# Expert tiles of 128 rows, the second matmul with the gelu's output stationary, its bias added at eviction

## The chip, the cores and the metric

The kernel runs on one core of a Trainium2 chip. The metric is the device time of one launch in microseconds. The array engine is TensorE (PE in the profile, its weight loads PEld), the others are VectorE (DVE), ScalarE (ACT), GpSimd (POOL) and SyncE (SP). A name with a q behind it (DVEq, SPq) stands for work of that engine's instruction sequencer: register arithmetic, waits, issues of DMAs.

## What is computed

Two transformer layers over 16 sequences of 256 tokens of width 128, in fp32. The first is attention with a band mask, then a mixture of experts; the second is attention with 16 small heads, then a recurrent cell. The change touches the mixture of experts alone:

```python
logits = -dist2 + x @ rw.T + rb              # 16 experts
topv, topi = lax.top_k(logits, 4)            # each token goes to 4 of them
w = softmax(topv)
hidden = gelu(x @ w1[e].T + b1[e])           # 128 -> 512
exp_out = hidden @ w2[e].T + b2[e]           # 512 -> 128
fused = sum over the 4 of w * exp_out
x = layernorm(x + fused)
```

## The kernel before

Each engine has its own program, written out by hand, and the engines meet at semaphores: `need(engine, name, count)` is a wait, `.then_inc` counts up. Loops are `batch_loop`, which writes the first and last turns out and leaves the middle to a loop of the engine's sequencer (its branch stands at L42).

The first stage is the attention of layer 0 with the routing. For each of the 4096 x 4 pairs of token and expert GpSimd scatters the token's row to `xs` in HBM, into the region of its expert. When all are counted, VectorE works out a plan (L1190 to L1231): the experts' regions are cut into tiles of GT = 256 rows, and for every tile `plan` holds the expert's number and the first row. The number of tiles is fixed, NT = 80, and those past the end run on a dummy region. SyncE and ScalarE write zeros behind each expert's last row (`pad`, L346). Meanwhile the weights of all experts lie in the on-chip array `wall`, per expert 516 columns of w1 and b1 (WA) and 513 of w2 and b2 (WB).

The expert stage then runs over tiles n. In a turn of the loop each engine does:

- SyncE: `load_rows(n + 2)`, 256 rows from `xs` to `xg`, after reading the row's number from `plan` (L389).
- TensorE: four matmuls up(n), w1 stationary and 256 columns of `xgT` moving (L766); two transposes of the rows of tile n + 1 (L748); four matmuls down(n - 1), w2 stationary and `hid` moving, into the bank DN (L774); two transposes of `yTe` of tile n - 2 back to rows (L780).
- ScalarE: four gelus of tile n (L993), then `yTe` = DN + b2, b2 being one value per partition (L997), then the store of tile n - 3 from `yrow` to `ys` (L984).
- VectorE: reads the expert's number of tile n + 1 from `plan` (L1240), copies its part of `wall` to `wA` (L1243), copies the transposed rows from PSUM to `xgT` (L1250), copies `wB` (L1246), and copies the rows of tile n - 2 from PSUM to `yrow` (L1291).

`wA`, `wB`, `hid`, `xg` and `yrow` have two buffers each. SyncE loads eight constants for the last stage (`cw_in`) in its first turn, and TensorE waits for them ahead of its second turn of the loop (L755). Behind the second turn VectorE runs `prepare()` (L1257), which ends with the comparison at L1271 that GpSimd waits for; GpSimd then rewrites positions and clears buffers, and clears one more (`clear(2)`, L532) once the last `wB` is copied, since that buffer lies inside `wall`. When `ys_out` says that all rows are stored, GpSimd gathers the rows of `ys` (L543), and the attention of layer 1 starts.

## Time and profile before

| | |
|---|---|
| median of 3 launches | 1743.43 us |
| lowest and highest | 1741.2 and 1749.72 us |
| span of the profiled execution | 1814.1 us |
| PE busy | 1434.0 us (79%) |
| PEld busy | 974.1 us (54%) |
| DVE busy | 1064.9 us (59%) |
| ACT busy | 973.5 us (54%) |
| POOL busy | 448.9 us (25%) |
| L766, 640 records, mean | 390 ns |
| L774, 640 records, mean | 379 ns |
| HBM read, written | 47.92 MB, 29.49 MB |

The profiled execution is 71 us longer than the median without a profile. For it only the span from the first to the last instruction is known, no launch time of its own. The table counts records: an fp32 matmul leaves two records and a transpose one. A record of a matmul has its end modelled, so the distance between starts tells more than the length.

### The profile page before, as it was taken

What the parts mean: (1) busy time and instruction counts of PE and PEld (TensorE: products, weight loads), DVE (VectorE), ACT (ScalarE), POOL (GpSimd) and SP (SyncE); (2) the same over time, 40 slices, a digit from 0 to 9 for tenths busy, and PEclk for the clock granted to TensorE, in tenths of its full rate; (3) what the DMA queues carried; (4) which work ended last, traced back from release to release, by engine and by line L of the source; (5) the groups of instructions that cost most, each with busy time, mean ns of one, the idle gap of its engine ahead of it and who ended that gap; (6) DMA issues with size and microseconds to landing.
All of it is one profiled execution on the core that took longest, in us unless ns stands there. A gap on an engine that the chain in (4) does not pass through costs nothing.

```text
span 1814.1 us, 32941 instructions
## 1 busy us (share of the span) xinstructions
PE 1434.0 (79%) x8094; PEld 974.1 (54%) x8094; DVE 1064.9 (59%) x3974; ACT 973.5 (54%) x2664; POOL 448.9 (25%) x495
## 2 busy tenths in 40 slices
PE   7999999999999999818999999125676667567581
PEld 4666665666665656416788888112344344335351
DVE  2677777777777777636443343025466556656555
ACT  6777777777777777414455555002344334334454
POOL 1012111222222212125100000665434433441003
PEclk9999999999999999859999999656788778878896
DMA  9000000000000000022122222144334333332301
GB/s 342 1 10 12 12 12 12 12 12 12 12 12 12 10 10 12 11 81 64 59 67 69 64 69 66 38 63 57 49 54 51 50 41 56 49 49 42 41 2 46
DMA packets 76443, 78.90 MB, mean 43 GB/s; under 512 B 10769, under 2 KB 69650, under 8 KB 75954
## 3 DMA queue, kind: packets, MB, share of 16 engines
q1 hardware_dynamic: 55378, 49.77, 13.9%
q0 software_dynamic: 8192, 16.79, 3.3%
q10 hardware_dynamic: 12816, 11.67, 1.9%
q8 instruction: 24, 0.39, 0.1%
q14 instruction: 33, 0.27, 0.1%
HBM read 47.92 MB, written 29.49 MB: 43 GB/s over the span
## 4 chain that ended last, share of the span: by engine, by line
PE 26%; DMA 11%; SPq 6%; issue 4%; DVE 3%; another core or an unknown queue 2%; ACT 1%; DVEq 1%; POOL 1%; POOLq 0%; ACTq 0%
PE psum L766 7%; PE psum L774 7%; DMA qst<-mrow 5%; SPq L425 3%; PE psum L810 3%; DMA wall<-mrow 3%; PE psum L799 2%; DMA qkd<-parts 2%; SPq L439 1%; PE psum L873 1%; PE psum L748 1%; PE psum L832 1%; PE psum L780 1%; POOL yk L543 1%
## 5 line engine op out<-in xcount | busy, mean ns | idle before, releaser
L947 ACT ACTIVATE P<-shifted,least 128x192 f32<-128x192 f32 (+1 forms) x512 | 240.9, 471 | 179.5 <-DVE least L1111 164.9
L1311 DVE TENSOR_REDUCE mx<-psum 128x2 f32<-128x512 f32 x256 | 165.6, 686 | 172.2 <-PE psum L873 128.3
L1010 ACT ACTIVATE wall<-psum 128x1024 f32<-128x1024 f32 x128 | 131.1, 1024 | 215.9 <-PE psum L799 153.2
L659 PE MATMUL psum<-kT,qT 128*128 128x384 f32 (+1 forms) x512 | 214.7, 542 | 0.0
L492 POOL DMA_INDIRECT xs<-x1c,pos x128 | 125.1, 978 | 335.2 <-DVE pos L1182 298.5
L1111 DVE CUSTOM_DVE_ANT_0 shifted<-psum,band 128x192 f32<-128x192 f32 (+1 forms) x512 | 170.6, 383 | 48.7 <-PE psum L659 32.9
L993 ACT ACTIVATE hid<-psum,wA 128x256 f32<-128x256 f32 x320 | 133.1, 471 | 66.3 <-PE psum L766 65.4
L766 PE MATMUL psum<-xgT,wA 128*128 128x256 f32 x640 | 157.5, 390 | 11.1 <-DVE xgT L1250 11.1
L674 PE MATMUL psum<-ident,P 128*128 128x128 f32 x1024 | 138.4, 278 | 18.7 <-DVE P L1104 18.6
L774 PE MATMUL psum<-hid,wB 128*128 128x256 f32 x640 | 151.4, 379 | 0.4 <-ACT yTe L997 0.4
L1104 DVE TENSOR_SCALAR P<-P,rinv 128x192 f32<-128x192 f32 (+1 forms) x512 | 145.1, 345 | 9.9
L674 PEld LDWEIGHTS psum<-ident,P 128*128 128x128 f32 x1024 | 116.2, 142 | 40.6 <-DVE P L1104 22.8
L543 POOL DMA_INDIRECT yk<-ys,posc x128 | 123.1, 962 | 48.9 <-issue 34.1
L766 PEld LDWEIGHTS psum<-xgT,wA 128*128 128x128 f32 x640 | 118.6, 195 | 26.7 <-issue 11.3
L774 PEld LDWEIGHTS psum<-hid,wB 128*128 128x128 f32 x640 | 115.5, 190 | 13.1 <-issue 0.6
L915 ACT ACTIVATE kT<-psum,cols 64x256 f32<-64x256 f32 x256 | 118.5, 463 | 3.2
L1246 DVE COPY wB<-wall 128x513 f32 x80 | 45.6, 570 | 126.0 <-ACT yTe L997 126.0
L659 PEld LDWEIGHTS psum<-kT,qT 128*128 128x128 f32 x512 | 95.8, 190 | 41.6 <-issue 1.4
L799 PE MATMUL psum<-qst,kst 128*128 128x256 bf16 x352 | 64.4, 315 | 57.3 <-DMA qst<-mrow 50.2
L947 ACT ACTIVATION_READ_ACCUMULATOR P<-shifted,least 128x1 f32 x512 | 95.6, 187 | 0.0
L1090 DVE TENSOR_TENSOR V<-psum,bv 128x512 f32<-128x512 f32 x62 | 42.8, 690 | 85.8 <-PE psum L619 61.3
L873 PE MATMUL psum<-kst,qst 128*128 128x256 bf16 x352 | 66.2, 314 | 30.1 <-DVE mx L1311 21.5
(244 smaller groups left out, 2649.6 us busy)
## 6 DMA issues: line engine op xcount, KB each, us to landing
xg<-xs SPq DMA_DIRECT2D x80, 128.0 KB, 2.0
ys<-yrow ACTq DMA_DIRECT2D x80, 128.0 KB, 1.7
wall<-in_wall SPq DMA_DIRECT2D x1, 8232.0 KB, 35.6
qkd<-parts SPq DMA_DIRECT2D x16, 384.0 KB
qst<-qkd SPq DMA_DIRECT2D x66, 64.0 KB
kst<-qkd SPq DMA_DIRECT2D x66, 64.0 KB
wall<-qkd SPq DMA_DIRECT2D x60, 64.0 KB
hT<-in_xT SPq DMA_DIRECT2D x4, 512.0 KB, 5.9
```

Source lines behind the costliest of these rows:

```text
L492: nc.gpsimd.indirect_dma_start(out=xs, out_offset=bass.IndirectOffsetOnAxis(pos[:, k:k + 1], 0), in_=x1c[:, k // TOPK, :], in_offset=None) ...
L543: g.indirect_dma_start(out=yk[:, n, :], out_offset=None, in_=ys, in_offset=bass.IndirectOffsetOnAxis(posc[:, n:n + 1], 0)).then_inc(s["yk_ ...
L659: mm(bk[:, 0:2 * w].rearrange("q (h j) -> q h j", h=2), qT[:, p, it * 128:(it + 1) * 128], kT[:, p, :, 0:w], start=True, stop=True).then_i ...
L674: last = nc.tensor.transpose(bk[:, c0:c0 + 128], P[:, par1, it, h, jt * 128:(jt + 1) * 128], ident[:, :])
L766: mm(UP[p][:, f * GT:(f + 1) * GT], wA[:, p, f * 128:(f + 1) * 128], xgT[:, p, :], start=True, stop=True).then_inc(s["up_mm"], 1)
L774: last = mm(DN[:, 0:GT], wB[:, q, f * D:(f + 1) * D], hid[:, q, f, :], start=(f == 0), stop=(f == FC - 1))
L947: last = sc.activation(P[:, par, it, h, 0:w], shifted[:, par, it, h, 0:w], ACT.Exp, scale=-1.0, bias=least[:, par, n:n + 1], accum_out=row ...
L993: sc.activation(hid[:, p, f, :], UP[p][:, f * GT:(f + 1) * GT], ACT.Gelu, bias=wA[:, p, F + f:F + f + 1]).then_inc(s["hid_ready"], 1)
L1010: sc.activation(pc[:, p % 4, :, :, :].rearrange("q h j n -> q (h j n)"), ST, ACT.Exp, scale=SCALE1).then_inc(s["exps1"], 1)
L1104: v.tensor_scalar(x, x, rinv[:, par1, n:n + 1], None, ALU.mult).then_inc(s["pn_ready"], 1)
L1111: v.tensor_tensor_reduce(out=shifted[:, par, it, h, 0:w], in0=bk[:, h * w:(h + 1) * w], in1=band[:, it, 0:w], scale=-SCALE0, scalar=3.0e38 ...
L1311: v.tensor_reduce(out=mx[:, :, h], in_=SB[(par + 1 + h) % 3].rearrange("q (i n) -> q i n", i=TT), axis=mybir.AxisListType.X, op=ALU.max).t ...
```

## The change

Tiles have 128 rows instead of 256, and NT is 144 instead of 80 (18,432 rows instead of 20,480). The loop is unrolled by four tiles, and `xg`, `wA`, `wB`, `hid` and `yrow` have four buffers. `yTe` and its transposes are gone: down(n - 2) has the gelu's output `hid` stationary and w2 moving, so rows of tokens come out, and DN has two banks. The bias b2 lies along the row there, so it is needed on all partitions: at the end of the first stage TensorE multiplies each expert's b2 column, broadcast to 128 columns, by the identity (16 products), and ScalarE copies the result into `wall` (4 copies), whose WB part grows from 513 to 640 columns. VectorE adds it while it moves DN to `yrow`. The stores go from ScalarE to SyncE, two tiles at a time. Pads write 128 rows, and the plan's arithmetic handles two columns of tiles.

The stages around it are otherwise the same. The diff, cut to its core:

```diff
-GT = 256
+GT = 128
-NT += NT % 2
+NT += -NT % 4
-WB = FC * D + 1
+WB = FC * D + D
```

SyncE:

```diff
-            load_rows(0, 0)
-            load_rows(1, 1)
+            def load_rows(n, buf):
+                need_alone(sp, "tin_mm", n - 3)
+                sp.dma_start(xg[:, buf, :], xs[bass.ds(row_of(n), GT), :]).then_inc(s[f"xg_in{buf}"], 16)
+            def store_rows(n, buf):
+                need_alone(sp, "yrow_ready", n + 2)
+                need_alone(sp, "ys_out", 8 * n)
+                sp.dma_start(ys[bass.ds(n * GT, 2 * GT), :].rearrange("(a p) d -> p a d", a=2), yrow[:, buf:buf + 2, :]).then_inc(s["ys_out"], 16)
+            for n in range(4):
+                load_rows(n, n)
             def body(i):
+                for p in range(4):
+                    n = 4 * i + p
+                    if is_tile(i, p, 4):
+                        load_rows(n + 4, p)
+                    if p % 2 == 1 and is_tile(i, p, -5):
+                        store_rows(n - 5, (p - 5) % 4)
                 if isinstance(i, int) and i == 0:
                     for dst, src in ((cw, "cw"), (lora_a, "lora_a"), (lora_b, "lora_b"), (gw, "gw"), (gu, "gu"), (gcol, "gcol"),
                                      (bo1, "bo1"), (bo2, "bo2")):
                         load(dst, src, "cw_in")
```

TensorE:

```diff
+            pe.wait_ge(s["wall_in"], 16)
+            for e in range(E):
+                b2 = wall[:, e, WA + FC * D:WA + FC * D + 1].to_broadcast([128, D])
+                mm(psum[:, e * D:(e + 1) * D], b2, ident[:, :], start=True, stop=True).then_inc(s["b2_mm"], 1)
...
+                    n, two = 4 * i + p, p % 2
                     if is_tile(i, p, 0):
                         need(pe, "xgT_ready", n + 1)
                         need(pe, "wA_ready", n + 1)
                         need(pe, "hid_ready", 4 * n - 4)
                         for f in range(FC):
-                            mm(UP[p][:, f * GT:(f + 1) * GT], wA[:, p, f * 128:(f + 1) * 128], xgT[:, p, :], start=True, stop=True).then_inc(s["up_mm"], 1)
+                            mm(UP[two][:, at:at + GT], wA[:, p, f * 128:(f + 1) * 128], xgT[:, two, :], start=True, stop=True).then_inc(s["up_mm"], 1)
                     if is_tile(i, p, 1):
-                        rows_in(n + 1, q, 16 * i + 16 * (p + 1))
-                    if is_tile(i, p, -1):
-                        need(pe, "yTe_ready", n - 1)
+                        rows_in(n + 1, (p + 1) % 4, 16 * (i + (p + 1) // 4) + 16)
+                    if is_tile(i, p, -2):
+                        need(pe, "hid_ready", 4 * n - 4)
+                        need(pe, "wB_ready", n - 1)
+                        need(pe, "yrow_ready", n - 3)
                         for f in range(FC):
-                            last = mm(DN[:, 0:GT], wB[:, q, f * D:(f + 1) * D], hid[:, q, f, :], start=(f == 0), stop=(f == FC - 1))
+                            last = mm(DN[two][:, 0:D], hid[:, m, f, :], wB[:, m, f * D:(f + 1) * D], start=(f == 0), stop=(f == FC - 1))
                         last.then_inc(s["dn_mm"], 1)
-                        for k in range(2):
-                            last = nc.tensor.transpose(TO[:, k * D:(k + 1) * D], yTe[:, p, k * 128:(k + 1) * 128], ident[:, :])
-                        last.then_inc(s["tout_mm"], 1)
```

ScalarE:

```diff
+            for k in range(0, E, 4):
+                act.wait_ge(s["b2_mm"], k + 4)
+                sc.copy(wall[:, k:k + 4, WA + FC * D:WCOLS], psum[:, k * D:(k + 4) * D].rearrange("q (e d) -> q e d", e=4))
             act.drain().then_inc(s["a_done"], 1)
...
-                        sc.activation(yTe[:, q, :], DN[:, 0:GT], ACT.Identity, bias=wB[:, q, FC * D:FC * D + 1]).then_inc(s["yTe_ready"], 1)
-                    if is_tile(i, p, -3):
-                        store(n - 3, q)
```

VectorE:

```diff
                     if is_tile(i, p, 1):
                         e = expert_of(n + 1)
                         need(dve, "up_mm", 4 * n)
-                        need(dve, "hid_ready", 4 * n)
+                        need(dve, "hid_ready", 4 * n - 8)
                         weights_A(e, q)
-                        rows_T(n + 1, q)
-                    if is_tile(i, p, -1):
-                        need(dve, "dn_mm", n)
-                        need(dve, "yTe_ready", n)
+                        rows_T(n + 1, q % 2)
+                    if is_tile(i, p, -2):
+                        m = (p - 2) % 4
+                        need(dve, "dn_mm", n - 1)
+                        need(dve, "ys_out", 16 * ((n - 4) // 2) if isinstance(n, int) else 32 * i + (16 * ((p - 4) // 2)))
+                        v.tensor_tensor(yrow[:, m, :], DN[p % 2][:, 0:D], wB[:, m, FC * D:FC * D + D], ALU.add).then_inc(s["yrow_ready"], 1)
                     if is_tile(i, p, 1):
+                        need(dve, "yrow_ready", n - 2)
                         weights_B(e, q)
-                    if is_tile(i, p, -2):
-                        need(dve, "tout_mm", n - 1)
-                        need(dve, "ys_out", 16 * n - 48)
-                        v.tensor_copy(yrow[:, p, :, :], TO[:, 0:GT].rearrange("q (a d) -> q a d", a=2)).then_inc(s["yrow_ready"], 1)
```

The order of VectorE inside the loop, before, from one copy into wB to the next copy of the rows and the wB behind it. `ISA` and `REGISTER_ALU` are steps of the sequencer, and the names in brackets are the semaphores that a step waits for:

```order
L1246 COPY wB<-wall 128x513
L294 REGISTER_ALU
L294 ISA [waits tout_mm]
L1291 COPY yrow<-psum 128x256 [waits ys_out]
L1240 ISA
L1240 TENSOR_LOAD plan
L1240 ISA x2
L294 REGISTER_ALU
L1243 ISA [waits hid_ready,up_mm]
L1243 COPY wA<-wall 128x516
L294 REGISTER_ALU
L1250 COPY xgT<-psum 128x256 [waits tin_mm]
```

And VectorE inside the loop after the change, from one yrow to the next wA:

```order
L298 ISA [waits dn_mm]
L1291 TENSOR_TENSOR yrow<-psum,wB 128x128 [waits ys_out]
L298 REGISTER_ALU
L1250 ISA [waits yrow_ready]
L1250 COPY wB<-wall 128x640
L1244 ISA
L1244 TENSOR_LOAD plan
L1244 ISA x2
L298 REGISTER_ALU
L298 REGISTER_ALU [waits up_mm]
L1247 ISA [waits hid_ready]
L1247 COPY wA<-wall 128x516
```

The copy into wB has moved behind yrow and waits for it, and the reading of `plan` (TENSOR_LOAD) now stands behind wB instead of behind yrow. The wait for ScalarE's yTe is gone.

TensorE inside the loop, one tile before the change:

```order
L294 ISA [waits wA_ready,xgT_ready]
L766 MATMUL psum<-xgT,wA 128x256 [waits hid_ready]
L766 MATMUL psum<-xgT,wA 128x256 x3
L294 REGISTER_ALU
L748 MATMUL psum<-ident,xg 128x128 [waits xgT_ready,xg_in0]
L748 MATMUL psum<-ident,xg 128x128
L774 MATMUL psum<-hid,wB 128x256 [waits yTe_ready,wB_ready,hid_ready]
L774 MATMUL psum<-hid,wB 128x256 x3
L780 MATMUL psum<-ident,yTe 128x128 [waits yrow_ready,yTe_ready]
L780 MATMUL psum<-ident,yTe 128x128
```

And one tile after it:

```order
L298 REGISTER_ALU
L298 ISA [waits wA_ready,xgT_ready]
L782 MATMUL psum<-xgT,wA 128x128 [waits hid_ready]
L782 MATMUL psum<-xgT,wA 128x128 x3
L764 MATMUL psum<-ident,xg 128x128 [waits xgT_ready,xg_in3]
L791 MATMUL psum<-wB,hid 128x128 [waits yrow_ready,wB_ready,hid_ready]
L791 MATMUL psum<-wB,hid 128x128 x3
```

One transpose and the two of yTe have gone, down waits for a yrow three tiles back and for no result of ScalarE that is newer than that of two tiles back, and up still waits for xgT and wA of its own tile.

## Rows read from the trace of the kernel before

**Rows 1.** Windows: length, busy time by engine (instructions), clock, DMA share, GB/s

```profile
900.00:920.00 20.00, 20.00 (x105) 17.34 (x104) 7.70 (x21) 11.26 (x27) 0.00 (x0) 1.00 0.23 70
```

**Rows 2.** Timeline of one tile: start, length, engine, line, count, idle before, releaser

```profile
950.37 0.42 DVE L1291 COPY yrow<-psum 128x256 f32<-128x256 f32 x1
...
951.24 1.89 PE L774 MATMUL psum<-hid,wB 128*128 128x256 f32 x8
...
951.40 0.43 DVE L1243 COPY wA<-wall 128x516 f32 x1 [0.61 <-ACT hid L993]
...
951.75 0.42 DVE L1250 COPY xgT<-psum 128x256 f32<-128x256 f32 x1
...
953.16 0.47 ACT L997 ACTIVATE yTe<-psum,wB 128x256 f32<-128x256 f32 x1 [1.11 <-PE psum L774]
...
953.18 1.89 PE L766 MATMUL psum<-xgT,wA 128*128 128x256 f32 x8
...
953.85 0.43 DVE L1246 COPY wB<-wall 128x513 f32 x1 [1.68 <-ACT yTe L997]
...
954.19 0.42 DVE L1291 COPY yrow<-psum 128x256 f32<-128x256 f32 x1
...
954.30 1.65 ACT L993 ACTIVATE hid<-psum,wA 128x256 f32<-128x256 f32 x4 [0.66 <-PE psum L766]
...
957.08 1.89 PE L766 MATMUL psum<-xgT,wA 128*128 128x256 f32 x8
```

**Rows 3.** Timeline: runs of 128-column fp32 records, two stages

```profile
500.37 1.04 PE L674 MATMUL psum<-ident,P 128*128 128x128 f32 x8
...
821.13 0.96 PEld L757 LDWEIGHTS psum<-lora_b,lora_a 16*128 16x128 f32 x8 [1.18 <-DMA bo<-in_bo]
```

**Rows 4.** L1240 in two tiles: count, min/median/max ns, first and last start

```profile
L1240 DVEq TENSOR_LOAD <-plan x1: 465/465/465, 950.4 to 950.4; - x1
...
L1240 DVEq TENSOR_LOAD <-plan x1: 321/321/321, 954.4 to 954.4; - x1
```

**Rows 5.** Groups of the page: busy, mean ns of one, idle before

```profile
L1090 DVE TENSOR_TENSOR V<-psum,bv 128x512 f32<-128x512 f32 x62 | 42.8, 690 | 85.8 <-PE psum L619 61.3
```

**Rows 6.** Timeline and L393: the start of the expert stage

```profile
809.27 0.42 DVE L1250 COPY xgT<-psum 128x256 f32<-128x256 f32 x1 [7.23 <-PE psum L748]
...
809.75 3.78 PE L766 MATMUL psum<-xgT,wA 128*128 128x256 f32 x8 [0.52 <-DVE xgT L1250]
...
822.21 1.99 PE L766 MATMUL psum<-xgT,wA 128*128 128x256 f32 x8
...
L393 SPq DMA_DIRECT2D xg<-xs x2: 342/364/387, 806.4 to 807.5; - x2
```

**Rows 7.** Timeline, windows and groups: preparation and the stretch with GpSimd

```profile
831.45 0.22 DVE L1259 CAST identb<-ident 128x128 bf16<-128x128 f32 x1
...
859.05 3.48 DVE L1243 COPY wA<-wall 128x516 f32 x1
...
858.64 3.61 POOL L504 MEMSET kst<- 3x4096 bf16 x1
...
835.90:869.40 33.50, 24.60 (x120) 20.32 (x120) 29.43 (x27) 12.90 (x30) 31.73 (x16) 1.00 0.14 47
...
L1246 DVE COPY wB<-wall 128x513 f32 x6 | 13.8, 2305 | 3.0 <-ACT yTe L997 3.0
...
L1243 DVE COPY wA<-wall 128x516 f32 x7 | 12.2, 1746 | 0.5 <-ACT hid L993 0.5
```

**Rows 8.** Windows and timeline: the end of the expert stage

```profile
1137.30:1144.70 7.40, 5.38 (x26) 4.11 (x25) 1.46 (x5) 2.59 (x6) 7.06 (x3) 1.00 0.15 52
...
1148.07 0.19 POOL L539 COPY posc<-pos_all 128x8 uint32<-128x8 uint32 x1 [3.49 <-DMA ys<-yrow]
```

**Rows 9.** Timeline and L349: between the first stage and the experts

```profile
808.57 0.66 PE L748 MATMUL psum<-ident,xg 128*128 128x128 f32 x2 [23.76 <-DMA xg<-xs]
...
L349 SPq DMA_DIRECT2D xs<-zrow x8: 3/328/333, 792.5 to 803.5; - x8
```

More of the change, by code:

```diff
@@ L758, in tiles @@
                     last.then_inc(s["lora_mm"], 1)
-                for p in range(2):
-                    n, q = 2 * i + p, 1 - p
+                for p in range(4):
+                    n, two = 4 * i + p, p % 2
                     if is_tile(i, p, 0):
@@ L1274, in tiles @@
             def tiles(i):
-                for p in range(2):
-                    n, q = 2 * i + p, 1 - p
+                for p in range(4):
+                    n, q = 4 * i + p, (p + 1) % 4
                     if is_tile(i, p, 1):
```

119 lines of the change are left out of this document (52 added, 67 removed).

## The prediction, made before the changed kernel was run

> **What bounds the kernel now.** I read the windows view first, then one tile of the expert stage in the timeline. The stage runs from about 810 to 1148 us of the profiled span. In it TensorE is busy all the time at a granted clock of 1.00 [rows 1], while VectorE is busy 38% and ScalarE 56% of the window 900 to 920. One tile of 256 rows takes 3.89 us: its first matmuls start at 953.18, those of the next at 957.08 [rows 2]. This is pure array work. A 256-column product is two records 0.216 us apart (8 records in 1.89 us, the last of them 0.38 long: 1.51 / 7), a transpose is 0.109 us [rows 3], and 16 x 0.216 + 4 x 0.109 = 3.89. Eighty tiles are 311 us; the other 27 us of the stage are its start, the preparation for the next stage, collisions with GpSimd, and its end.
>
> The second thing to see is VectorE's own pace. The profile puts the wait of the copy into wA down to the gelu (L993), but the gelu it needs is that of the tile before, long done. wA starts 1.03 us behind the start of yrow (950.37 to 951.40), and between them stands the reading of the expert's number: a load from `plan` into a register of 0.47 us (0.32 in the next tile), then register arithmetic and waits [rows 4]. VectorE's sequencer does that serially. Today 3.89 us hide it.
>
> **The array work.** After the change a tile of 128 rows has 16 records of 128 columns and one transpose. Would a record take half the time? The nearest rows: eight transposes with eight stationary tiles take 1.04 us, (1.04 - 0.27) / 7 = 0.110 each; the weight loads of real fp32 128-column products follow one another at (0.96 - 0.19) / 7 = 0.110, right behind a wait [rows 3]. So a record costs 0.109, half of 0.216, and weight loading is just hidden. A tile is 17 x 0.109 = 1.85 us, 144 of them 267 us against 311: an array-only saving of 44 us. It comes from 18,432 instead of 20,480 rows and from the transposes of the output that fall away. ScalarE loses yTe and the store; four gelus of 128 columns cost at most the 1.65 us that four of 256 take [rows 2], and start two tiles ahead of their reader, so they set nothing. SyncE gets the stores: two loads and one store per two tiles, some 3.2 us by the spacing of its first loads (806.4 and 807.5 [rows 6]) and less for a store, under 4.4. Four row buffers give the landings, 2.0 us, three tiles of time.
>
> **VectorE's work per tile.** The wide copies do not halve: wA stays 516 columns, wB grows from 513 to 640 (0.43 to about 0.50). What halves is xgT: two like rows, 0.42 for 256 columns from PSUM and 0.69 for 512 [rows 2, 5], give about 1 ns a column above some 0.155, so 0.285. The new yrow, an addition from PSUM, is priced by the 512-column addition: 0.69 - 0.40 = 0.29 [rows 5]. No engine is full by that: 0.29 + 0.50 + 0.43 + 0.285 = 1.5 us. But they are chained.
>
> **The loop that I expect to set the pace.** Follow one turn, U being the first matmul of a tile. (1) Up, transpose and down: the last record of down starts 16 x 0.109 = 1.74 later and lasts 0.27: 2.01. (2) VectorE waits on `dn_mm` with an instruction of its sequencer, then issues yrow: 0.12 (the row of wB starts 0.21 behind its releaser yTe [rows 2], with two such waits). (3) yrow: 0.29. (4) wB now waits for `yrow_ready`, one sequencer step: 0.14. (5) From the start of wB to that of wA: the register chain, 1.03 in [rows 2]; and the load from `plan` ends in both tiles only behind the copy in front of it, at 950.82 and 954.7 behind 950.79 and 954.61 [rows 2, 4], which behind a copy of 0.50 makes 1.11. (6) xgT follows wA by 0.35, and lasts 0.285. (7) TensorE sees it: 0.06 at the first tile (809.69 to 809.75 [rows 6]), up to 0.2 where a sequencer step stands between; I take 0.13, and 0.10 for a first weight load that nothing hides (1.99 instead of 1.89 for eight records at 822.21 [rows 6]). Sum: 2.01 + 0.12 + 0.29 + 0.14 + 1.11 + 0.35 + 0.285 + 0.13 + 0.10 = 4.54 us. This loop goes round once in two tiles, since xgT of tile n + 2 follows yrow of tile n - 2 issued in tile n's turn: **2.27 us a tile** against 1.85 of array work. VectorE alone, without TensorE in the loop, takes 0.29 + 0.14 + 1.11 + 0.35 + 0.25 = 2.14.
>
> **The start.** Tile 4 waits for `cw_in` as tile 2 does now. SyncE issues those eight loads behind the rows of tile 7, which want the transpose of tile 3. At the half clock with which the stage opens (eight records in 3.78 us [rows 6]) I get: transpose of tile 3 at 817, last load issued at 822, landed at 824.2, four products of the loras, tile 4 at 825.3. Now tile 2, the same row, starts at 822.21. TensorE has then been idle 4 us and opens at the half clock again: 1.8 us.
>
> **Preparation and GpSimd.** The preparation occupies VectorE for 4.4 us (831.45 to 835.9, when GpSimd sets in [rows 7]). Then come 16 GpSimd instructions, 835.9 to 869.4. A wB or wA issued during one lasts until it ends: wA 3.48 us under the memset of 3.61 [rows 7]. (The Trainium skill, SBUF — State Buffer, in its part on engine ports, says that the pair of ports shared by VectorE and GpSimd is an exclusive lock held for a whole instruction; the trace agrees.) Before, 13 copies ran in these 33 us, 6.5 tiles of 256, with means of 1.75 and 2.31 us [rows 7]. Where each copy again pays one GpSimd instruction, 8 small tiles pass instead of 15, a loss of 15 us; where wA slips in behind wB before GpSimd takes its turn, about 5. I take 10.
>
> **The end.** After the last up come 1.85 us, then two more downs, yrow, and two stores that wait for each other: about 7 us. But `clear(2)` waits for the last wB, now 0.9 us behind the last up, and takes 7.3 us (three GpSimd instructions, 1137.3 to 1144.7 [rows 8]): 8.3 us until the first gather.
>
> **Ahead of the stage.** The 16 products that spread b2 and the four copies on ScalarE start where TensorE now falls idle, 23.8 us ahead of the first transpose at 808.57 [rows 9]; at half clock 32 x 0.213 = 6.8 us, so ScalarE's nine pads begin 2.4 us late and still end with SyncE's, whose last is issued at 803.5, 18.7 us later [rows 9]. Nothing, or 1 us. Later stages are the same code.
>
> **Sum.** 825.3 + 1.8 + 139 x 2.27 + 4.4 + 10 = 1157.0 for the last up, + 8.3 = 1165.3 for the first gather, against 1148.1 in [rows 8]: **+17 us**. The profiled span is 1814.1 us, so it would be 1831. The median without a profile is 1743.4, 71 us less; the array-bound tiles can't hold that difference, so it lies in chains. A stage that becomes a chain may be a few us shorter unprofiled. I leave that to the range: 1743.4 + 17 = **1760 us**.
>
> **Rivals.** (A) TensorE stays the bound, 1.85 us a tile: 139 x 0.42 = 58 us less, 1702. For it: no engine's own work exceeds 1.85. Against it: 1.03 us of sequencer time is in every tile of the trace and everything near it is serial. 10%. (B) The sequencer steps overlap more than I think, or the load from `plan` doesn't wait for wB, and the pace is VectorE's own, about 2.12: 21 us less, 1739. 25%. (C) Slower for another reason: TensorE cannot issue small pairs fast enough once its queue runs dry at each wait. At 0.124 instead of 0.109 a record the loop grows by 0.24, to 2.39 a tile, + 17: 1777; it decides from 0.055 us an instruction upward. Against it, the eight weight loads behind a wait at 0.110 [rows 3]. 10%. (The Trainium skill, TensorE: Matmul & The Clock Gate, Part 1, gives about 62 ns of sequencer work per matmul where decoding is done in software; by it this rival would hold. No run here shows it.) (D) The 0.4 us gap in each tile brings the clock down to the 1.2 GHz level: the array part of the loop doubles, 139 x 0.9 = 125 us more, 1885. Against it, the stretch with GpSimd has TensorE busy 73% at a clock of 1.00 [rows 7]; here it is 82%. 5%.
>
> **How the numbers follow.** The forecast has 50%, with 1745 to 1778 as its own range (GpSimd 5 or 15, pace 2.2 to 2.35). About 0.5% (8.7 us) is what a measurement can tell from no change. Faster than 1734.7: A and a third of B, 0.19. Within: the rest of B and a fifth of the forecast, 0.28. Slower: the rest of the forecast, C, D, 0.53. The range 1726 to 1780 leaves out A and D and the edge of C.
>
> **What the profile will show.** Right: up matmuls of successive tiles 2.2 to 2.35 apart, idle time of TensorE ended by xgT, wA 1.0 to 1.15 behind wB, no copy of VectorE waiting for ScalarE. A pace of 1.85 or 2.12 with TensorE never waiting for xgT would make step 5 wrong; records over 0.109 apart would show C. In the stretch with GpSimd, count how many wA and wB last over a microsecond.

## The result, and the profile of the changed kernel

The changed kernel takes 1752.28 us (median of 20 runs, 1746.71 to 1765.29), the kernel before 1745.66 us (20 runs on the same chip, 1735.64 to 1754.97). The ratio is 1.0043 with a 95% interval of 1.0026 to 1.0060: slower by 0.4%, on the edge of what a measurement tells from no change. The forecast was 1760 us, in a range from 1726 to 1780. Its sign and its main mechanism hold. Two of its terms do not, by 19 us and by 12 us, and their errors have opposite signs. Most of this text is about these two.

Two groups of the page of the changed kernel (line, engine, operation, count | busy us, mean ns of one | idle time before, and what ended most of it), and one of its list of waits (total us, times, longest):

```profile
L782 PE MATMUL psum<-xgT,wA 128*128 128x128 f32 x1152 | 171.9, 295 | 24.2 <-DVE xgT L1254 21.6
...
L1247 DVE COPY wA<-wall 128x516 f32 x144 | 73.7, 512 | 82.1 <-ACT hid L1003 45.8
```

```profile
PE psum L782 <- DVE xgT L1254: 21.6, 31, 3.7
```

TensorE now waits for VectorE's copy of the transposed rows, as forecast; before, it had no such wait in the steady part. Of the 21.6 us in the list, 16.5 are six waits in the stretch with GpSimd. From 900 to 1100 us, 94 tiles, the list has 15 such waits with 2.5 us, and against them 56 waits of VectorE's yrow for the down product, 20.9 us: the two engines wait for each other in turn. The profile again puts most of VectorE's idle time ahead of wA (46 of 82 us in 144 tiles) down to the gelu, and again, as in [rows 2], the gelu is innocent: the experiments below show whose time it is.

The windows view of the changed kernel, same columns as [rows 1], the same stretch, the one in which GpSimd has work, and three windows of 7 us within it:

```profile
900.00:920.00 20.00, 19.63 (x162) 18.44 (x161) 12.25 (x37) 10.74 (x38) 0.00 (x0) 1.00 0.20 58
...
819.50:853.30 33.80, 20.51 (x102) 19.48 (x102) 31.86 (x27) 7.41 (x24) 32.08 (x16) 0.70 0.08 24
```

```profile
827.00:834.00 7.00, 6.79 (x34) 6.74 (x34) 5.06 (x8) 2.50 (x8) 6.32 (x7) 0.55 0.10 29
834.00:841.00 7.00, 2.40 (x20) 2.08 (x18) 7.00 (x8) 1.15 (x4) 6.77 (x4) 0.93 0.13 37
841.00:848.00 7.00, 5.17 (x23) 4.88 (x24) 7.00 (x5) 1.28 (x5) 6.77 (x3) 0.50 0.03 9
```

In steady state TensorE is busy 98% by the modelled ends of its records. That share hides most of what TensorE loses, on average 0.23 us a tile; the distance between starts does not. One turn of the loop that the prediction followed, in the timeline of the changed kernel (start, length, engine, line):

```profile
1001.79 1.15 PE L782 MATMUL psum<-xgT,wA 128*128 128x128 f32 x8 [0.17 <-DVE xgT L1254]
...
1002.89 1.06 PE L791 MATMUL psum<-wB,hid 128*128 128x128 f32 x8
...
1004.09 0.29 DVE L1291 TENSOR_TENSOR yrow<-psum,wB 128x128 f32<-128x128 f32 x1 [0.36 <-PE psum L791]
1004.31 0.49 DVE L1250 COPY wB<-wall 128x640 f32 x1
...
1005.34 0.43 DVE L1247 COPY wA<-wall 128x516 f32 x1 [0.54 <-ACT hid L1003]
1005.68 0.28 DVE L1254 COPY xgT<-psum 128x128 f32<-128x128 f32 x1
...
1006.10 1.15 PE L782 MATMUL psum<-xgT,wA 128*128 128x128 f32 x8
```

The load of the expert's number between wB and wA, one turn earlier (count, min/median/max ns, first and last start):

```profile
L1244 DVEq TENSOR_LOAD <-plan x1: 307/307/307, 1000.1 to 1000.1; - x1
```

From the up product of one tile (1001.79) over down (ends 1003.95), yrow (1004.09), wB (1004.31), wA (1005.34), xgT (1005.68 to 1005.96) to the up product two tiles on (1006.10) it is 4.31 us. The first ups of successive tiles are 2.23, 2.07, 2.24 and 1.99 apart, again and again: 2.131 us a tile, against a forecast of 2.27, with 2.2 to 2.35 as its bounds, and an array work that the experiments put at 1.90.

How the kernels compare. "Stage" is from the first up product to the first gather, "end" from the last up to the first gather, all from each kernel's own trace. Each ratio is to the kernel before on the same chip in the same session. The changed kernel was timed in a session of its own, so a difference between it and an experiment compares two sessions, and so does one between most pairs of experiments; by the ratios it can come out some us away from the difference of the medians. The chip of e_rows256_one and e_ahead_8 is slower in the stages around the experts (the kernel before took 1807 us there), so of these two only the ratio and the stage say something.

| kernel | us | ratio to before (95%) | stage | us a tile | end |
|---|---|---|---|---|---|
| before (e_before) | 1750.6, one run | | 342.4 | 3.895 | 12.9 |
| changed | 1752.28 | 1.0043 (1.0026 to 1.0060) | 348.3 | 2.131 | 9.5 |
| e_read_ahead | 1742.69 | 0.9969 (0.9950 to 0.9988) | 338.3 | 2.049 | 9.5 |
| e_read_twice | 1803.16 | 1.0336 (1.0307 to 1.0365) | 397.9 | 2.513 | |
| e_before_twice | 1746.59 | 1.0003 (0.9984 to 1.0021) | 340.6 | 3.895 | |
| e_rows256 | 1729.55 | 0.9901 (0.9876 to 0.9926) | 324.8 | 3.734 | 11.3 |
| e_one_copy | 1762.28 | 1.0088 (1.0056 to 1.0119) | 359.6 | 2.298 | 8.3 |
| e_ahead_one | 1741.44 | 0.9970 (0.9951 to 0.9989) | 340.2 | 2.145 | 8.3 |
| e_clears_late | 1763.37 | 1.0098 (1.0066 to 1.0130) | 354.1 | 2.130 | 30.7 |
| e_rows256_one | 1787.25 | 0.9892 (0.9868 to 0.9916) | 320.0 | 3.734 | 11.3 |
| e_ahead_8 | 1798.27 | 0.9952 (0.9933 to 0.9970) | 329.4 | 1.988 | 9.5 |
| e_rows256_short | 1719.40 | 0.9827 (0.9796 to 0.9857) | 316.1 | 3.734 | 11.2 |
| e_ahead_8_short | 1725.21 | 0.9864 (0.9839 to 0.9888) | 323.3 | 1.988 | 9.0 |

### The profile page after: what moved, and what is told of

It reads as the page before. It is cut to its first block, busy times and chain, and to the rows that moved or that the text cites. A ratio compares the mean times of both kernels' runs of the same rounds, so it can differ in the third digit from the quotient of the medians.

```text
span 1756.7 us, 36578 instructions
## 1 busy us (share of the span) xinstructions
PE 1404.2 (80%) x8974; PEld 992.4 (56%) x8974; DVE 1136.9 (65%) x4231; ACT 969.6 (55%) x2844; POOL 447.3 (25%) x495
## 4 chain that ended last, share of the span: by engine, by line
issue 20%; DMA 10%; PE 9%; SPq 6%; DVE 3%; POOL 3%; POOLq 3%; ACT 1%; DVEq 1%; ACTq 0%
DMA qst<-mrow 5%; SPq L437 3%; DMA wall<-mrow 3%; POOL yk L555 2%; PE psum L821 2%; PE psum L810 2%; DMA qkd<-parts 2%; PE psum L884 1%; SPq L451 1%; SPq L439 1%; POOLq L517 1%; PE psum L782 1%; PE psum L843 1%; PE psum L900 1%; DVE parts L1396 0%
## 5 line engine op out<-in xcount | busy, mean ns | idle before, releaser
L1003 ACT ACTIVATE hid<-psum,wA 128x128 f32<-128x128 f32 x576 | 165.6, 368 | 172.5 <-PE psum L782 172.4
L782 PE MATMUL psum<-xgT,wA 128*128 128x128 f32 x1152 | 171.9, 295 | 24.2 <-DVE xgT L1254 21.6
L782 PEld LDWEIGHTS psum<-xgT,wA 128*128 128x128 f32 x1152 | 147.5, 200 | 41.6 <-issue 35.9
L791 PE MATMUL psum<-wB,hid 128*128 128x128 f32 x1152 | 156.6, 281 | 0.0
L791 PEld LDWEIGHTS psum<-wB,hid 128*128 128x128 f32 x1152 | 144.9, 198 | 0.0
L1247 DVE COPY wA<-wall 128x516 f32 x144 | 73.7, 512 | 82.1 <-ACT hid L1003 45.8
```

The costliest lines, as they stand in the source:

```text
L782: mm(UP[two][:, at:at + GT], wA[:, p, f * 128:(f + 1) * 128], xgT[:, two, :], start=True, stop=True).then_inc(s["up_mm"], 1)
L791: last = mm(DN[two][:, 0:D], hid[:, m, f, :], wB[:, m, f * D:(f + 1) * D], start=(f == 0), stop=(f == FC - 1))
L1003: sc.activation(hid[:, p, f, :], UP[two][:, at:at + GT], ACT.Gelu, bias=wA[:, p, F + f:F + f + 1]).then_inc(s["hid_ready"], 1)
```

## The experiments

The theory: the tile's pace is set by a chain that goes through VectorE and the reading of the expert's number (the register read, for short), and the rest of the loss is GpSimd holding VectorE's copies. The rival to its first half: the pace comes of something that the small tile does to TensorE, VectorE's copies or the stores, and the register read is only an innocent row in between.

### The kernel before, once more (e_before)

> The kernel before, unchanged, for a second profile to set beside that of the changed kernel. Theory 1 (the time went inside the expert stage: a gain of the array lost to VectorE's chain and to GpSimd): the stage from the first up to the first gather is again 338 us, against 347 in the changed kernel, and the stretch between the last mask product of the first stage and the first up is again 25 us against 22. Theory 2 (the 57 us by which its first profile was longer lie in the expert stage): the stage comes out shorter than 330 us.

Measured: span 1748.8 us, launch 1750.6 us; 3.895 us a tile, as in [rows 2]. That lies inside the 1740 to 1757 us of the other 22 launches of this kernel in the same session, so the profile costs no time that one execution can show. The 71 us more of the profile of before are not in the expert stage either: that stage took 339 us there and 342 here, the stages around it took more. The prediction put those 71 us down to chains that run shorter without a profile, and this run gives that no support. What they resemble is the slower chip of e_ahead_8: there too the first up comes at 812.5 us (809.8 in the profile of before, 789.1 here) and the mean granted clock is 0.896 (0.895, and 0.912 here). From the first gather to the end the profile of before is longer still, 665.0 against 651.7 us, and which chip it was taken on is not on record, so this stays open.

### The number read one tile ahead (e_read_ahead)

```diff
+                ahead = None
...
-                        e = expert_of(n + 1)
+                        e = expert_of(n + 1) if ahead is None else ahead
...
                         rows_T(n + 1, q % 2)
+                        ahead = expert_of(n + 2) if p < 3 and is_tile(i, p, 2) else None
```

> The changed kernel, with the expert's number of the next tile read from plan right behind the copy into xgT instead of behind wB, for three tiles of four. Theory 1 (the loop through VectorE's register chain sets the pace of 2.13 us a tile): wB to wA falls from 0.96 to about 0.42 us in those three, TensorE with 1.90 us becomes the bound there, the pace is 1.95 to 2.0, and the kernel is 18 to 25 us faster than the changed one: about 1730. Theory 2 (small records and waits of TensorE itself set the pace, and the chain is beside the path): no change, 1752.

Timeline of this kernel, a tile with its number read ahead, and the tile behind the loop's branch, whose number is still read in place:

```profile
1002.53 0.48 DVE L1250 COPY wB<-wall 128x640 f32 x1
...
1002.93 0.42 DVE L1247 COPY wA<-wall 128x516 f32 x1
...
1003.93 1.06 PE L782 MATMUL psum<-xgT,wA 128*128 128x128 f32 x8
...
1004.34 0.48 DVE L1250 COPY wB<-wall 128x640 f32 x1
...
1005.56 0.43 DVE L1247 COPY wA<-wall 128x516 f32 x1 [0.74 <-ACT hid L1003]
...
1006.32 1.15 PE L782 MATMUL psum<-xgT,wA 128*128 128x128 f32 x8 [0.34 <-DVE xgT L1254]
```

Where the number is there already, wA starts 0.40 us behind wB; where it is read in place, 1.22 us, and the same wait is still ascribed to the gelu. The ups are 1.99, 1.90, 1.90 and 2.40 apart. So 1.90 us is the array's own pace, and the read, with the branch in one tile of four, is the cause of what lies above it. The gain is 10 us of the stage and 9.6 us of time (13 by the ratios). The expectation named 1730, from a pace of 1.95 to 2.0; it is 2.049, because the fourth tile, which keeps the read and the branch, takes 2.40 and was priced too low.

### The number read twice (e_read_twice, e_before_twice)

```diff
                         e = expert_of(n + 1)
+                        e_B = expert_of(n + 1)
...
-                        weights_B(e, q)
+                        weights_B(e_B, q)
```

> The changed kernel with the expert's number read twice for each tile, once for wA and once for wB. Theory 1: the chain grows by about 0.6 us a tile, VectorE's own turn is then 0.21 + 1.65 + 0.35 + 0.29 = 2.5 us, the pace goes from 2.13 to 2.45 to 2.5 and the time up by 45 to 53 us: about 1800. Theory 2: within 5 us of 1752.

> The kernel before with the expert's number read twice for each tile of 256 rows. Theory 1 says that the same chain is there and hidden: VectorE sits idle 1.7 us ahead of wB in each tile, the 0.6 us more fit in, the pace stays 3.89 and the time 1745. Theory 2 says the same. A rise of 40 us or more would say that the read costs time by itself, on or off the path.

The same edit in both kernels. Timeline of the changed kernel with it, then of the kernel before with it, and that kernel's window:

```profile
1001.77 0.48 DVE L1250 COPY wB<-wall 128x640 f32 x1
1003.25 0.43 DVE L1247 COPY wA<-wall 128x516 f32 x1 [1.00 <-ACT hid L1003]
```

```profile
1000.19 0.42 DVE L1292 COPY yrow<-psum 128x256 f32<-128x256 f32 x1
1001.93 0.43 DVE L1243 COPY wA<-wall 128x516 f32 x1 [1.33 <-ACT hid L993]
```

```profile
900.00:920.00 20.00, 20.00 (x104) 17.39 (x103) 7.62 (x20) 11.19 (x27) 0.00 (x0) 1.00 0.20 66
```

In both the idle time ahead of wA grows by half a microsecond or more (0.54 to 1.00 and 0.61 to 1.33), and both times it is ascribed to the gelu, which nothing was done to. In the changed kernel it costs 0.38 us a tile, 55 us for 144 tiles, 51 us of time; in the kernel before, whose wA starts 1.74 us behind yrow instead of 1.03, it costs nothing: 1.0003. That is the difference between the tile sizes in steady state in one pair of numbers: a register read that 3.9 us hide, and 2.1 us don't. The rival is out.

### Tiles of 256 rows, with the rest of the change (e_rows256)

```diff
-GT = 128
+GT = 256
...
-                        for f in range(FC):
-                            last = mm(DN[two][:, 0:D], hid[:, m, f, :], wB[:, m, f * D:(f + 1) * D], start=(f == 0), stop=(f == FC - 1))
+                        for k in range(2):
+                            for f in range(FC):
+                                last = mm(DN[two][:, k * D:(k + 1) * D], hid[:, m, f, k * 128:(k + 1) * 128], wB[:, m, f * D:(f + 1) * D], start=(f == 0), stop=(f == FC - 1))
```

> The changed kernel with tiles of 256 rows as before: second matmul with the gelu's output as stationary side, bias at the eviction, stores of two tiles, but 80 tiles instead of 144. It tells the part of the change that the tile size is from the rest. Theory 1 (the other three parts pay, the small tile eats it: a tile of 256 rows has room for VectorE's chain, which costs about 2.1 us of 3.7): the array has two transposes, 16 records of 256 columns and 16 records of 128 columns, about 3.67 us against the 3.895 us of before, so 80 tiles save about 18 us, less cold tiles and GpSimd's stretch as before; with the shorter end (about 9.5 us from the last first matmul to the first gather against 12.9) and the 1 us ahead of the stage the kernel takes about 1728 us, pace 3.65 to 3.75 us per tile. Rival (the new orientation or the stores themselves cost time, and the small tile is what holds it near even): pace stays at 3.85 to 3.9 us and the kernel takes 1742 us or more.

Measured 1729.55 us and 3.734 us a tile: the expectation to 2 us. Its window, in which TensorE is full as in [rows 1] and VectorE has slack:

```profile
900.00:920.00 20.00, 20.00 (x143) 18.70 (x143) 8.47 (x21) 8.49 (x21) 0.00 (x0) 1.00 0.24 72
```

This splits the change. Against the kernel before, the second matmul with `hid` stationary, the bias at the eviction, the stores of two tiles and the four buffers, which this run doesn't take apart, give 1%: 0.161 us x 80 tiles = 13 us of array work, mostly the transposes of `yTe` that are gone, and the rest at the stage's end and start. The tile size alone then takes 1.4% back. It was to give 25 us (80 x 3.734 - 144 x 1.90) and cost 23.

### GpSimd's stretch: fewer copies, or no memsets (e_one_copy, e_clears_late)

```diff
-                v.tensor_copy(wA[:, par, :], wall[:, bass.ds(e, 1), 0:WA].rearrange("q o c -> q (o c)")).then_inc(s["wA_ready"], 1)
+                v.tensor_copy(wAB[:, par, :], wall[:, bass.ds(e, 1), :].rearrange("q o c -> q (o c)")).then_inc(s["wA_ready"], 1)
...
+                        need(dve, "yrow_ready", n - 2)
...
-                        weights_B(e, q)
```

> The changed kernel with an expert's numbers brought over in one VectorE copy of 1156 columns, at the place of the first of the two. Theory 1 (in GpSimd's stretch each copy between two SBUF tiles ends only when GpSimd's instruction of that moment ends, so the number of copies counts): in the stretch from 819.5 to 853 us a tile is held up once and not twice, and the about 22 us that the stretch loses fall to about 11 to 13. In steady state the copy of 0.85 us stands in the chain from one yrow to the next, where 0.43 stood, and the copy of the second matmul's numbers no longer delays the step before it by 0.2: about 0.1 us per tile longer, pace 2.2 to 2.25 us, +12 us. Sum about 1753 us, in two terms that the trace shows apart. Rival (GpSimd's busy time itself is what is lost, whatever the copies are cut into): the stretch still loses 20 us or more, and the kernel takes about 1764 us.

```diff
+            pool.wait_ge(s["wB_ready"], NT)
             for k in range(2):
                 clear(k)
             g.memset(zst[:, :, :], 0.0)
...
-            pool.wait_ge(s["wB_ready"], NT)
             clear(2)
```

> The changed kernel with GpSimd's memsets of the buffers that it shares with nobody's work at that time (22.7 us of instructions, 830.6 to 853.3 us) moved behind the last tile; its sums (819.5 to 830.5 us) stay. The order of work alone is changed. Theory 1 (those memsets hold VectorE's copies): the tiles after 831 us run at the steady pace of about 2.13 us at once, the stretch's loss falls from about 22 us to about 7 (what the sums cost), and the memsets now stand bare between the last tile and the first gather: 8.4 us there become about 31. Sum -15 + 22.7, about 1760 us; the stage up to the last first matmul about 15 us shorter. Rival (the stretch is slow for another reason, for instance the tiles' first rows or the stores): it stays slow when the memsets are gone, and the kernel takes about 1775 us.

First the stretch as it is in the changed kernel, GpSimd's instructions and VectorE's copies of weights in the timeline:

```profile
834.59 3.61 POOL L516 MEMSET kst<- 3x4096 bf16 x1
835.07 3.49 DVE L1250 COPY wB<-wall 128x640 f32 x1
838.32 1.98 POOL L513 MEMSET qst<- 128x2048 f32 x1
838.47 2.10 DVE L1247 COPY wA<-wall 128x516 f32 x1
840.24 2.08 POOL L514 MEMSET kst<- 128x2048 f32 x1
...
840.89 1.77 DVE L1250 COPY wB<-wall 128x640 f32 x1
842.43 3.68 POOL L516 MEMSET kst<- 3x4096 bf16 x1
842.59 3.81 DVE L1247 COPY wA<-wall 128x516 f32 x1
```

Read the pairs: a copy that takes 0.48 or 0.43 us elsewhere ends 0.3 to 0.4 us behind the end of GpSimd's instruction (838.56 behind 838.20, 840.57 behind 840.30), and before the next copy is issued GpSimd has the next instruction running. Of the 12 copies that start from 820.0 to 850.1, 11 last over a microsecond. From 820.0 to 856.9 seven tiles pass where 7 x 2.13 us would do, a loss of 22 us. (The Trainium skill, SBUF — State Buffer, Who interferes with whom, says that the order of issue and not an operation's shape decides which of the two waits, and that the loser blocks fully; the trace agrees: the copies that start behind an instruction of GpSimd wait, and GpSimd's memset of 2048 values grows only from 1.80 to 2.1 us.)

With one copy, the rows of the same pair:

```profile
840.11 2.25 POOL L513 MEMSET qst<- 128x2048 f32 x1
...
841.21 1.76 DVE L1246 COPY wAB<-wall 128x1156 f32 x1 [0.21 <-DVE yrow L1287]
```

Here eleven tiles pass between the yrow of 820.09 and that of 856.78, a loss of 36.7 - 11 x 2.30 = 11.4 us: half, as expected. It is the count of copies that pays, though not it alone, perhaps: in this run TensorE's granted clock is 1.00 from 834 to 848, where it is 0.50 to 0.93 in the changed kernel. But the kernel is 10 us slower than the changed one and 9 us slower than expected: 0.76 us of copy now stand in the chain where 0.43 stood, and the tile takes 2.298 us and not the 2.2 to 2.25 that I had put down, 0.167 x 144 = 24 us. The mechanism in the stretch was shown; the price in the steady part I had too small by half.

With the memsets moved, the window that opens 4 us behind GpSimd's last sum is nearly a steady one:

```profile
834.00:841.00 7.00, 6.59 (x57) 6.22 (x56) 4.09 (x13) 3.80 (x14) 0.00 (x0) 1.00 0.17 48
```

The first two tiles behind GpSimd's sums take 2.44 and 2.42 us and the next ones 2.13 on average, the last up comes 15.2 us sooner than in the changed kernel (1111.9 against 1127.1), the stretch keeps the loss of GpSimd's sums (11.5 us for two tiles, so 7.3), and the end grows from 9.5 to 30.7 us. Expected were -15, +22.7 and 1760 us; measured -15, +21 and 1763.4, of which 5 us are not in the stage (354.1 against 348.3 explains 6 of the 11). So the 22 us of loss come with GpSimd's work, 15 of them with its memsets: held copies, and TensorE's lower clock between them. One of the two tiles under the sums is TensorE's own pace at that clock (3.78 us, without a wait), and no run here takes the two apart.

### Both edits (e_ahead_one)

This is e_one_copy with the read ahead of e_read_ahead.

> Both edits together: the expert's number read one tile ahead and one copy of 1156 columns. Theory 1 (the two act on different terms, and the chain with the register read out of it has 0.3 us of room under the array's 1.9): steady tiles stay near the array's 1.90 us, three of four, and the one that crosses the loop's branch takes about 2.4, pace 2.03 to 2.1 us; GpSimd's stretch loses 11 to 13 us instead of about 22. Sum 1742.7 with the read ahead alone, less 10, plus 0 to 5: about 1735 us. Rival (the 0.42 us that the longer copy puts into the chain shows in every tile): pace 2.15 us or more and 1745 us or more.

A miss for theory 1. The time (1741.44) is 6 us over it and 4 under the rival, and the pace, 2.145, is the rival's but for 0.005. The tiles are 2.5 to 2.6, 1.99, 1.91 and 2.1 apart, so two of four are late. One place to look is the read, which now stands ahead of yrow (the second view is the register load, count and min/median/max ns, first and last start):

```profile
1006.39 0.29 DVE L1250 COPY xgT<-psum 128x128 f32<-128x128 f32 x1
1007.40 0.29 DVE L1289 TENSOR_TENSOR yrow<-psum,wAB 128x128 f32<-128x128 f32 x1 [0.72 <-DMA ys<-yrow]
```

```profile
L1243 DVEq TENSOR_LOAD <-plan x1: 502/502/502, 1006.5 to 1006.5; - x1
```

The idle time ahead of yrow is ascribed to a store, but the load of the next number runs in it, from 1006.50 to 1007.00, and its register steps until 1007.3. So the read was moved from one place in VectorE's serial program to another that can be on the chain as well. How much it costs there is less plain. The last record of the down product starts at 1006.98, and yrow 0.42 us behind it; in the changed kernel, where no read stands ahead of yrow, it is 0.31 to 0.42. In the tile behind the branch, which reads one number in place and the next one ahead, yrow comes 0.55 to 0.69 behind that record, so there the read costs 0.1 to 0.4 us. The rest is the rival's term: from yrow to xgT it is 0.21 + 0.40 + 0.33 us in e_read_ahead and 0.50 + 0.68 here, with the copy of 0.76 us. No run takes these shares apart.

### A loop of eight tiles (e_ahead_8), and one copy with 256 rows (e_rows256_one)

```diff
-                for p in range(4):
-                    n, q = 4 * i + p, (p + 1) % 4
+                for p in range(8):
+                    n, q = 8 * i + p, (p + 1) % 4
...
-            batch_loop(dve, 2, NT // 4 - 1, 2, tiles)
+            batch_loop(dve, 1, NT // 8 - 1, 2, tiles)
```

> The changed kernel with the expert's number read one tile ahead, as e_read_ahead (1742.7 us, pace 2.05), and VectorE's loop body of eight tiles instead of four. In e_read_ahead three tiles of four run at the array's 1.90 to 1.99 us, and the one behind the loop's branch, which reads its number in place, takes 2.40. Theory 1 (read and branch are all that is left of the chain's excess): one tile of eight takes 2.4 us, pace (2.40 + 1.99 + 6 x 1.90) / 8 = 1.97 us, 144 tiles save about 11 us, sum about 1732 us. Rival (the 2.40 us comes of other engines' loops, whose bodies stay at four tiles, so it returns every fourth tile): pace 2.03 to 2.05 us and no gain, about 1743 us.

> Tiles of 256 rows with the other three parts of the change (as e_rows256, 1729.6 us, pace 3.734), and an expert's numbers brought over in one VectorE copy. Theory 1 (a tile of 256 rows has room in VectorE's chain, so the longer copy costs nothing in steady state, and in GpSimd's stretch, where e_rows256 lost about 13 us over seven tiles to two held copies each, one is held): pace stays at 3.73 us, the stretch loses 5 to 8 us, sum about 1723 us. Rival (what the stretch loses there is set by how long GpSimd is busy, or the tile of 256 rows has no room for the copy): 1729 us or more.

In e_ahead_8 the ups are 2.53, 1.99 and six times 1.90 apart: 1.988, near the 1.97 expected. The late tile comes with VectorE's branch, every eighth, while the other engines' loops stay at four: the rival is out. The stage is 9 us shorter than in e_read_ahead. The ratio, 0.9952 of 1807 us, is -8.7 us, and against the 339.4 us of this stage in the profile of before the shorter stage alone makes -10. From e_read_ahead's 0.9969 it fell by 0.0017, where 9 us would be 0.005, and the intervals of the two overlap: the pace is shown by the traces, the gain in time from one to the other is not settled.

In e_rows256_one the pace stays at 3.734, and with the tile of the preparation the stretch loses 5 us (ten tiles in 42.0 us against 37.3) where e_rows256 lost 13: both as expected by theory 1. The ratio, -19.5 us, fits the stage (320.0 against 339.4), but is hardly below that of e_rows256 (0.9892 and 0.9901): 4 of the 8 us went into two slow tiles at the stage's start (7.8 and 6.5 us, against 6.7 and 3.8), and the intervals are wider than the rest.

### Shorter memsets (e_rows256_short, e_ahead_8_short)

```diff
+PAIR_OF_ONES = (2 ** 23 + 0x3F80) / 2 ** 23
...
-                g.memset(kst[k][MROW:MROW + NPART, :, :], 1.0)
+                g.memset(kst[k][MROW:MROW + NPART, :, :].rearrange("q h n -> q (h n)").bitcast(fp32), PAIR_OF_ONES)
...
-            g.memset(zst[:, :, :], 0.0)
+            g.memset(zst[:, :, :].rearrange("q h n -> q (h n)").bitcast(fp32), 0.0)
```

> As e_rows256_one (tiles of 256 rows, the other three parts of the change, one copy of an expert's numbers; ratio to the kernel before 0.989), and GpSimd's four memsets of 3x4096 values of two bytes (3.6 us each) written as 2048 values of four bytes with the same bits. Three of them stand in GpSimd's stretch, one bare between the last tile and the first gather. Theory 1 (a memset's time goes by its values per partition, and a held copy lasts until GpSimd's instruction ends): each takes about 1.8 us, the end shortens by 1.7 us, and the stretch by 1 to 3 us of the 4.7 that it still lost: ratio about 0.987. Rival (the time goes by bytes): 3.6 us as before and a ratio of 0.989.

> As e_ahead_8 (tiles of 128 rows, number read ahead, loop body of eight; ratio 0.9952), with the same shorter memsets. Theory 1: three of the longest holders of VectorE's copies lose 1.8 us each, and in this stretch, where each instruction of GpSimd holds one copy and a tile has two, nearly all of it shows: about 4 us, and 1.7 at the end: ratio about 0.992. Against e_rows256_short it says which tile size is ahead once VectorE's chain is out of the way: theory 1 says 256 rows by 0.5%, since the stretch holds both copies of each small tile. Rival (the stretch's time goes by bytes, or by the tiles): ratio 0.995.

GpSimd at the end of the stage, with tiles of 256 rows, without and with the edit (two kernels):

```profile
1107.45 3.50 POOL L516 MEMSET wall<- 3x4096 bf16 x1
```

```profile
1095.59 1.80 POOL L517 MEMSET wall<- 3x2048 f32 x1
1103.97 0.19 POOL L552 COPY posc<-pos_all 128x8 uint32<-128x8 uint32 x1 [6.58 <-DMA ys<-yrow]
```

A memset goes by its values per partition and not by its bytes: 4096 values of two bytes take 3.50 us, 2048 of four bytes 1.80, on 3 partitions as on 128. With tiles of 128 rows the stage falls by 6.1 us, near the 5.7 expected, 5.4 of them in the stretch and 0.5 at the end. With tiles of 256 it falls by 3.9, but 3.5 of these stand in the first five tiles, ahead of GpSimd's work, where the edit does nothing (the second tile takes 2.79 us and not 4.73, the fifth 5.35 and not 6.49); the stretch gives 0.5 and the end nothing. At the end posc waits for the last stores in both, so the 1.7 us expected there were on the path for 0.5 us at most. Both ratios came out lower than expected, 0.9827 for 0.987 and 0.9864 for 0.992, which is -30 and -24 us. Against the 339 to 342 us of the stage before, the stages of the two account for 23 to 26 and 16 to 19 of these; the rest lies outside the expert stage, and I can't place it. The order of the two is as expected, 256 rows ahead by 0.3%, but their intervals overlap; e_rows256_short beats both kernels of this case clearly, by 1.7% and 2.1%. How much of that the shorter memsets give is not shown: in the stage of this kernel it is half a microsecond.

## Why the prediction was right, and where it was wrong

**What bounds the kernel, and the loop: right.** The stage turned from array work into the loop over VectorE, with the register read as its largest serial piece. e_read_ahead, e_read_twice and e_before_twice show it by taking away and doubling it. The warning that the profile's releaser of wA (the gelu) is not the cause held as well. Of the signs named for the profile, TensorE's wait for xgT came; the ups stand 1.99 to 2.24 apart and not 2.2 to 2.35, and wA 0.95 to 1.23 behind wB and not 1.0 to 1.15.

**The size of the loop: 2.27 forecast, 2.131 measured, 19 us over 139 tiles.** Step by step, in the turn shown above: step 1, up to down, 2.16 for 2.01; step 2, 0.14 for 0.12; steps 3 and 4, from yrow to wB, 0.22 for 0.43; step 5, wB to wA, 1.03 for 1.11 (0.95 to 1.23 in the four tiles of a turn); step 6, 0.34 + 0.28 for 0.35 + 0.285; step 7, 0.14 for 0.23. The step that failed is step 4. I read `need(dve, "yrow_ready", n - 2)` as a wait for the yrow just issued, in the prediction and in the section on the change; the count is that of the yrow before it, done long ago. So wB starts while yrow still runs, and yrow and the wait are 0.22 us and not 0.29 + 0.14. That is 0.21 us a turn, 0.105 a tile, 15 of the 19 us; the other steps make up the rest. A wait's count has to be worked out like an address: which instruction raises the semaphore to that number.

**Rival B, by its number nearly the winner.** It named 2.12 us, and 2.131 was measured, closer than my 2.27 (its time, 1739, was farther off, since it had the same 10 us for GpSimd's stretch). One of its conditions came true, sequencer steps that overlap more than I thought: the wait ahead of wB runs under yrow. Its mechanism did not: with VectorE bound by its own work its yrow would never wait for TensorE, but it does in 56 of 94 tiles, for 20.9 us, 0.22 a tile. Without these waits VectorE would need about 1.9 us a tile, an estimate from these two numbers, and TensorE alone needs 1.90. It is the loop through both that takes 2.13, as forecast, with a step less in it.

**The array work: 1.85 forecast, 1.90 measured.** In e_read_ahead the tiles that wait for nothing are 1.90 apart. The weight loads of the eight products stand 0.1115 us apart ((0.97 - 0.19) / 7) where [rows 3] had 0.110, and there are 17. Rival A would have been 1709 and not 1702.

**GpSimd's stretch: 10 forecast, with 5 to 15 for a range, 22 measured.** The mechanism was the one named, a copy waits for GpSimd's instruction, but I counted instructions (16, so 8 tiles) where held copies have to be counted. Four sums of 1.3 us pass under three copies and two short instructions (0.5 and 0.3 us) under none; 12 copies in all, so six tiles, are issued from 820.0 to 850.1 us, a seventh behind them: seven tiles in 37 us and not eight in 33. A second thing came on top, and it is rival D in small: in the stretch TensorE's granted clock fell to the level of 1.2 GHz (0.55 and 0.50 in two of the windows above), where it works for 2 to 4 us and idles for 1 to 4 between tiles; the stretch of the kernel before had 1.00 [rows 7], and e_rows256 has 1.00 there too. Much of that is hidden behind the held copies, but not all. In the window 827 to 834 TensorE is busy for 6.79 of 7.00 us and VectorE for 5.06, and from 827.22 to 831.00 a tile takes 3.78 us. Another takes 3.50 when GpSimd is done already, at 853.26:

```profile
853.39 1.78 PE L782 MATMUL psum<-xgT,wA 128*128 128x128 f32 x8 [2.81 <-DVE xgT L1254]
...
856.89 1.19 PE L782 MATMUL psum<-xgT,wA 128*128 128x128 f32 x8
```

Against 2.13 each, these two are up to 3 of the 22 us, an estimate. Rival D priced the low clock at every tile and named no such stretch.

**Start, preparation, end, ahead of the stage: right.** Tile 4 started 15.6 us behind the first up (forecast 15.5). The tiles behind it took 3.79 and 2.71 instead of 2.13 each, 2.2 us (forecast 1.8). The preparation cost 3.7 us (5.82 for a tile; forecast 4.4). From the last up to posc it is 8.4 us (forecast 8.3), and `clear(2)` ends it, as said:

```profile
1127.10 1.10 PE L782 MATMUL psum<-xgT,wA 128*128 128x128 f32 x8
...
1127.51 0.48 DVE L1250 COPY wB<-wall 128x640 f32 x1
...
1128.05 1.81 POOL L513 MEMSET wall<- 128x2048 f32 x1 [274.78 <-DVE wB L1250]
...
1131.72 3.50 POOL L516 MEMSET wall<- 3x4096 bf16 x1
1135.55 0.19 POOL L551 COPY posc<-pos_all 128x8 uint32<-128x8 uint32 x1 [0.33 <-issue]
```

Ahead of the stage the kernel is 0.9 us quicker (22.1 us from the last product of the routing to the first up, 23.0 in e_before). Forecast was nothing or 1.

**The sum.** From the first up to posc the forecast has 355.5 us, the trace 347.2: 19 less for the loop, 12 more for the stretch, and smaller things. Against [rows 6, 8], where it is 338.3, that makes 9 us, against e_before 6, less 1 ahead of the stage, for 6.6 measured. The forecast said +17, 10 us too much, and 1760, 8 us too much, and it came that near by luck: two errors of 19 and 12 us partly cancelled. Both terms, the pace and the stretch, lay outside their own bounds, so the range deserved less trust than the hit suggests. Two small slips of the working change nothing: the upper end of its own range, 1778, is 1776 by its terms, and the three chances of faster, within and slower should be 0.18, 0.27 and 0.55.

## What to carry to other kernels

Halving a tile halves what goes by rows and nothing that goes by tiles: register reads, weight copies, waits, held ports. Add up those per tile in their serial order before the array's saving is counted, and look in the trace for instructions of the sequencer between two rows of an engine, since the engine's idle time there is put down to whichever semaphore it last looked at. Here the parts of the change that had nothing to do with the tile size were worth 1%, and trying them alone would have been the better first step.

## What the runs showed of the hardware that I had not expected

- A copy with a register in its address starts 0.55 to 0.8 us later where the number is read right ahead of it: wB to wA is 0.40 us with the number there (the copy of wB itself lasts 0.48), 0.95 to 1.03 us with it read in place and 1.22 behind the loop's branch; the load from `plan` is 0.31 of it, and a second read adds 0.5 (1.48). A load took 0.50 us in one tile of e_ahead_one (1006.50 to 1007.00), while xgT was copied.
- GpSimd's memset goes by values per partition: 3x4096 of two bytes 3.50 us, 3x2048 of four bytes with the same bits 1.80, 128x2048 of four bytes 1.80.
- The granted clock fell in a stretch in which TensorE was busy 61% (20.51 of 33.80 us, mean clock 0.70), in pieces of 2 to 4 us with 1 to 4 us of idle time between, while e_rows256 kept 1.00 in its own stretch with GpSimd.
- The kernel before took 3.3 to 3.5% longer on another chip (1807.29 us against 1745.66 to 1749.47), and nothing of it shows in the expert stage's pace: 3.734 us a tile on both chips with 256 rows, 1.988 on both with 128 and the loop of eight. The first up comes at 812.5 us there and at 788.5 here (e_ahead_8, e_ahead_8_short), and from the first gather to the end it is 651.7 us against 619.5. Why, no trace of mine says; TensorE's mean granted clock in the profiles was 0.896 to 0.898 there and 0.905 to 0.917 elsewhere.
